# The far path's tables loaded during the last batch, and four of six lead rows evicted by VectorE, in a two-block convolution kernel

## The reference

```
x = x + L0(group_norm(x))     # two 3x3 conv branches, each times a sigmoid attention map
x = x + L1(group_norm(x))     # modulated deformable 3x3 convolution, batch norm, relu

def L1(x):                                    # K*K = 9 taps
    off_y, off_x = conv3x3(x, offset_w)       # one offset per tap and pixel
    mask = 2 * sigmoid(conv3x3(x, mod_w))
    sy, sx = off_y + row + tap_y, off_x + column + tap_x
    sampled = bilinear(x, sy, sx) * mask      # zero outside the image
    out = einsum('nckhw,ock->nohw', sampled, weight) + bias
    out = (out - mean) * rsqrt(var + 1e-5)    # over batch and pixels
    return relu(out * gamma + beta)
```

## Time and profile before

| | us |
|---|---|
| runs, median (lowest to highest of 3) | 423.75 (423.46 to 424.14) |
| profiled execution | 425.59 |
| its span | 423.8 |

### The profile page before, as it was taken

The page is one execution under the profiler, slowest core; times in us unless marked ns, Lnnn a source line. Parts: engine busy times, 40 slices in busy tenths (PEclk is TensorE's granted clock), DMA queues, the critical chain, the costliest instruction groups (busy, mean ns, idle before and its releaser), DMA issues.

```text
span 423.8 us, 14386 instructions
## 1 busy us (share of the span) xinstructions
PE 313.0 (74%) x6057; PEld 203.1 (48%) x6058; DVE 319.8 (75%) x625; ACT 252.8 (60%) x380; POOL 204.3 (48%) x242
## 2 busy tenths in 40 slices
PE   0079999848747419899989989898998999870470
PEld 0022334312213106777757777677775777760460
DVE  5456267833689852999979999799999799993266
ACT  1023322405047108888888888788888888880355
POOL 9770000199491001666646665556666466656000
PEclk9999999969679558999999999999999999996565
DMA  7799200178580643300011001001100000000005
GB/s 226 131 234 239 48 2 0 26 212 235 128 208 9 128 97 90 97 28 3 29 29 44 6 28 28 29 11 40 29 29 26 4 5 3 3 4 19 2 0 198
DMA packets 18106, 28.65 MB, mean 68 GB/s; under 512 B 6890, under 2 KB 7465, under 8 KB 18029
## 3 DMA queue, kind: packets, MB, share of 16 engines
q1 hardware_dynamic: 12397, 19.40, 17.1%
q0 software_dynamic: 2400, 5.07, 5.2%
q10 hardware_dynamic: 3246, 3.27, 3.5%
HBM read 8.03 MB, written 5.83 MB: 33 GB/s over the span
## 4 chain that ended last, share of the span: by engine, by line
PE 42%; ACT 28%; DVE 8%; DMA 7%; SPq 6%; issue 5%; ACTq 1%; POOL 1%; DVEq 1%; POOLq 0%
ACT hx L931 17%; PE ps L641 10%; PE ps L771 9%; ACT zreg L1014 8%; PE ps L584 6%; PE ps L605 5%; PE ps L654 4%; DMA hx<-xpad 3%; SPq L440 3%; PE ps L595 2%; SPq L345 2%; ACT zreg L999 2%; PE ps L780 1%; DMA x_sb<-in_x 1%; DVE x_sb L1397 1%
## 5 line engine op out<-in xcount | busy, mean ns | idle before, releaser
L561 POOL TENSOR_TENSOR prod<-prod 128x416 f32<-128x416 f32 x128 | 134.9, 1075 | 119.4 <-DVE prod L1311 119.4
L1311 DVE TENSOR_TENSOR prod<-ps,hy 128x480 f32<-128x480 f32 (+1 forms) x256 | 137.6, 600 | 23.7 <-PE ps L780 20.9
L780 PE MATMUL ps<-zreg,hx 64*64 64x96 f32 x4608 | 113.1, 247 | 0.0
L931 ACT ACTIVATE hx<-ps 128x576 f32<-128x576 f32 x131 | 78.2, 648 | 49.2 <-PE ps L771 28.5
L780 PEld LDWEIGHTS ps<-zreg,hx 64*64 64x64 f32 x4608 | 101.0, 132 | 7.5
L1018 ACT ACTIVATE hx<-hx,rbias 128x1152 f32<-128x1152 f32 x64 | 81.1, 1267 | 0.0
L1319 DVE TENSOR_REDUCE areg<-prod 128x32 f32<-128x448 f32 x128 | 72.7, 608 | 0.5 <-POOL prod L561 0.4
L641 PE MATMUL ps<-preg,sel 26*128 26x288 bf16 x260 | 42.4, 281 | 31.0 <-ACT zreg L1014 18.1
L771 PE MATMUL ps<-wzp,sreg 128*128 128x144 bf16 x512 | 43.1, 227 | 0.0
L641 PEld LDWEIGHTS ps<-preg,sel 26*128 26x128 bf16 x260 | 19.9, 91 | 46.5 <-issue 31.0
L1014 ACT ACTIVATE zreg<-ps 128x576 f32<-128x576 f32 x64 | 42.1, 658 | 0.0
(11 more groups left out here) (178 smaller groups left out, 354.9 us busy)
## 6 DMA issues: line engine op xcount, KB each, us to landing
scratch<-zreg SPq DMA_DIRECT2D x12, 240.0 KB, 4.2
sreg<-scratch SPq DMA_DIRECT2D x12, 192.0 KB, 2.5
out<-x_sb SPq DMA_DIRECT2D x8, 256.0 KB, 2.1
x_sb<-in_x SPq DMA_DIRECT2D x3, 512.0 KB, 4.9
areg<-xpad POOLq DMA_DIRECT2D x23, 66.0 KB, 3.6
areg<-xpad SPq DMA_DIRECT2D x23, 66.0 KB, 2.7
sreg<-scratch SPq DMA_DIRECT2D x4, 336.0 KB, 3.3
zreg<-xpad POOLq DMA_DIRECT2D x15, 66.0 KB, 4.1
```

Source lines behind the costliest of these rows:

```text
L561: pool.tensor_tensor(slots[:, :, 0:2 * moved], slots[:, :, 0:2 * moved], slots[:, :, 2 * KEPT:6 * KK], ALU.add).then_inc(folded, 1)
L780: return pe.matmul(g_ps(g, h)[u * W:(u + 1) * W, k - TAPS[h][0], :, :], hx[s, (t + u) % 4, k, :], z_sb[s, y + u + k // 3:y + u + k // 3 + ...
L931: act.activation(hx[:, t % 4, :, :].rearrange("p k (h x) -> p h k x", h=2), dist_ps(bank).rearrange("p h (k x) -> p h k x", k=KK), ACT.Abs)\
L1311: mul = vector.tensor_tensor(pv[:, n0:n1], gv, wv[:, n0:n1], ALU.mult)
```

## The change

`far_tab` now begins at column 0 of `zreg`, in z rows 0 to 7. POOL clears it in four pieces of 544 columns, one after the folds of each of the pairs 54 to 57. These are pairs 6 to 9 of the last batch, which work on row 12 and later, so rows 0 to 7 are no longer read. SyncE's six loads wait for four pieces. As `out_t` now overlaps the tables, ScalarE waits for `far_loaded` ahead of its first output eviction. Of the six lead rows of a batch, VectorE evicts the first four (`lead_rows`, counted by `lead_low`), and ScalarE the last two (`lead_saved`).

```diff
--- before.py
+++ after.py
@@ -156,7 +156,7 @@
         xparts = zflat[:, ZSLOTS * KW - NPART * ZSLOTS * W:ZSLOTS * KW].bitcast(bf16)\
             .rearrange("p (q n) -> p q n", q=NPART)
         xrest = prod[:, :, :].rearrange("p a n -> p (a n)")[:, HH * B * KK:HH * B * KK + ZPIECE * P128]
-        far_tab = zflat[:, NPIX:NPIX + B * KW + 2 * B * P128]
+        far_tab = zflat[:, 0:B * KW + 2 * B * P128]
         wz_far = far_tab[:, 0:B * KW].rearrange("p (b n) -> p b n", b=B)
         sel_far = far_tab[0:SELK, B * KW:].bitcast(bf16).rearrange("p (e n) -> p e n", n=P128)
         out_t = zflat[:, 0:NPIX]
@@ -241,6 +241,7 @@
         zrow_saved = sem("zrow_saved")
         lead_made = sem("lead_made")
         lead_saved = sem("lead_saved")
+        lead_low = sem("lead_low")
         dist_made = sem("dist_made")
         dist_ready = sem("dist_ready")
         g_ready = sem("g_ready")
@@ -310,6 +311,7 @@
             return ps[:, (bank + u) * BANK:(bank + u) * BANK + KW]
 
 
+        DVE_LEADS = 4
         LEAD_BANKS = (0, 0, 2, 2, 0, 0)
 
         def pair(row):
@@ -356,6 +358,7 @@
 
         FAR = H + 2
         FAR1 = 128
+        FAR_PIECES = 4
 
         def far_rows(eng, tile, turn):
 
@@ -473,7 +476,7 @@
                     sync.wait_ge(xs_loaded, b * (32 * NQ) + 32 * q)
                     sync.sem_inc(load_turns, 1)
                     load_piece(b, q)
-            sync.wait_ge(far_zeroed, 2)
+            sync.wait_ge(far_zeroed, FAR_PIECES)
             for b in range(B):
                 sync.dma_start(wz_far[b * C:(b + 1) * C, b, :], d["wz"]).then_inc(far_loaded, 16)
             for h in range(2):
@@ -560,10 +563,11 @@
                     moved = 3 * KK - KEPT
                     pool.tensor_tensor(slots[:, :, 0:2 * moved], slots[:, :, 0:2 * moved], slots[:, :, 2 * KEPT:6 * KK],
                                        ALU.add).then_inc(folded, 1)
-
-            pool.wait_ge(acc_ready, NT)
-            pool.memset(far_tab[:, 0:B * KW], 0.0).then_inc(far_zeroed, 1)
-            pool.memset(far_tab[:, B * KW:], 0.0).then_inc(far_zeroed, 1)
+                piece = i - (NT // 2 - HH // 2 + 6)
+                if 0 <= piece < FAR_PIECES:
+                    n = (B * KW + 2 * B * P128) // FAR_PIECES
+                    pool.memset(far_tab[:, piece * n:(piece + 1) * n], 0.0).then_inc(far_zeroed, 1)
+
             pool.wait_ge(reach_ready, 2)
 
             pool.wait_ge(px_ready, 16 * (1 + 3 * PX_DMAS))
@@ -748,7 +752,7 @@
                 for j in range(ZLEAD):
                     if j >= 4:
 
-                        pe.wait_ge(lead_saved, b * ZLEAD + (j - 3))
+                        pe.wait_ge(lead_low, b * DVE_LEADS + (j - 3))
                     z_row(j, j % 2, LEAD_BANKS[j]).then_inc(lead_made, 1)
                 for y in range(0, HH, 2):
                     t = b * HH + y
@@ -761,7 +765,8 @@
                     pe.wait_ge(dist_ready, t + 3)
                     pe.wait_ge(zrow_saved, t + CREDIT)
                     if y == 0:
-                        pe.wait_ge(lead_saved, (b + 1) * ZLEAD)
+                        pe.wait_ge(lead_low, (b + 1) * DVE_LEADS)
+                        pe.wait_ge(lead_saved, (b + 1) * (ZLEAD - DVE_LEADS))
                     for u in range(2):
                         distance((t + 2 + u) // HH, (t + 2 + u) % HH, PAIR_BANKS[u])
 
@@ -994,7 +999,7 @@
             for b in range(B):
 
                 act.wait_ge(xparts_stored, 16 * B * (NQ - 1))
-                for j in range(ZLEAD):
+                for j in range(DVE_LEADS, ZLEAD):
                     act.wait_ge(lead_made, b * ZLEAD + (j + 1))
                     act.activation(z_sb[:, j, :], z_ps(j % 2, LEAD_BANKS[j]), ACT.Copy).then_inc(lead_saved, 1)
                 for y in range(0, HH, 2):
@@ -1040,6 +1045,8 @@
             act.activation(warm[:, 5:6], warm[:, 0:1], ACT.Sqrt).then_inc(warmed, 1)
             for c in range(NCH):
                 act.wait_ge(outt_made, c + 1)
+                if c == 0:
+                    act.wait_ge(far_loaded, 16 * (B + 2))
                 act.activation(out_t[:, c * BANK:(c + 1) * BANK], ps[:, (c % 4) * BANK:(c % 4 + 1) * BANK],
                                ACT.Identity, bias=vec[:, V_DBIAS:V_DBIAS + 1]).then_inc(outt_saved, 1)
             root(4)
@@ -1320,9 +1327,18 @@
                                      .rearrange("p (a n e) -> p a e n", a=C // 2, e=2)[:, :, :, 0:KEPT],
                                      AX.X, ALU.add).then_inc(acc_ready, 1)
 
+            def lead_rows(b):
+
+                for j in range(DVE_LEADS):
+                    vector.wait_ge(lead_made, b * ZLEAD + (j + 1))
+                    vector.tensor_copy(z_sb[:, j, :], z_ps(j % 2, LEAD_BANKS[j])).then_inc(lead_low, 1)
+
+            lead_rows(0)
             for i in range(NT // 2):
                 weigh(i, 0)
                 weigh(i, 1)
+                if (i + 1) % (HH // 2) == 0 and i + 1 < NT // 2:
+                    lead_rows((i + 1) // (HH // 2))
                 if i > 0:
                     add_up(i - 1, 0)
                     add_up(i - 1, 1)
```

## The result

| kernel | median of its runs (lowest to highest) | ratio to before | profiled execution, span |
|---|---|---|---|
| before, same chip | 423.94 (423.46 to 428.67) | 1 | 425.59, 423.8 |
| after | 420.41 (417.69 to 424.10) | 0.9874 (0.9825 to 0.9923) | 424.10, 422.3 |

The kernel is faster by 1.26%, with an interval of about 0.5% to either side; 419.4 us and 1.0% were forecast. All ratios here are taken over undisturbed runs alone, which leaves out the profiled execution of after (424.10, the slowest of its four). The quotient of the two medians is 420.41 / 423.94 = 0.9917, so the size of the gain is known less well than the first number suggests.

A forecast was written before the change was run, and what follows sets the result against it. The prediction took a chain of waits as the bound, ScalarE and TensorE alternating in the pair loop, the tail waiting for its tables. Early tables -4.82 and lead rows +0.45 made -4.37: 423.75 to 419.4 us, range 417.8 to 421.2.

The forecast's parts named there:

- the case's own: Whole kernel: the narrower range given for the main forecast itself, 418.9 to 420.0 us, chance 65%.
- TensorE's path after the last reduce: Entry to far loop: last reduce ends 384.23, loop entry 385.35, `L808` at 386.17, `L818` at 387.33.
- The register work's 0.82: TensorE's far-loop entry: 0.82 us of sequencer work before the first matmul, kept from behind the table's landing.
- POOL's path: Far-loop staging: POOL's sequencer enters at about 381.55, as the last folds start; its twelve copies end 5.49 later, at 387.04.
- Forecast slack 0.3: At `L818`: POOL's copies end at 387.04, 0.3 us ahead of TensorE's 387.33, so TensorE decides.
- Rival A: Far-loop staging: last folds hold POOL's sequencer, copies end 388.0 to 389.1, tail gain only 4.1 to 3.05; 13%.
- Part 1's additions: Last batch: four memsets in POOL's idle 1.14, SyncE's six DMAs near 364 and one ScalarE wait cost zero.
- Lead rows: Batch boundaries: VectorE evicting four of six rows costs +0.15 us at each of three, +0.45 in sum; first batch zero.
- 0.12 to its end in PSUM and 0.12 to ScalarE's start: Batch boundary: estimated handover of TensorE's lead row 5 to ScalarE's eviction, after two matmuls of 0.15.
- The price of a copy: VectorE's lead-row eviction at a boundary: 288 columns take 0.45 us, spaced 0.367 apart, 0.067 above the columns.
- Rival B: Tail: TensorE's full clock returns sooner, output chunks gain a further 0.7 to 1.0 us, giving 418.5; 14%.
- everything behind `L818` moves as a block: Tail: all work after `L818` shifts by the same amount, so the gain there is 4.82 us.

The follow-up runs named there:

- e7: The changed kernel with POOL's wait for all 128 reductions put back ahead of its far loop, no memset there; 422.40 us, ratio 0.9972.
- e8: The changed kernel with TensorE entering the far loop once VectorE's last multiply has freed PSUM, not after the last reduce; 420.53 us, ratio 0.9920.
- parts 1 and 2 alone: Two kernels against before: only the early tables, 419.62 us (ratio 0.9872); only VectorE's lead-row evictions, tables late, 425.19 us (ratio 1.0010).
- e4: The changed kernel with 24 unused matmuls over 26 rows, 512 columns, in TensorE's wait ahead of the first distances; 421.77 us, ratio 0.9921.
- part 1 alone: Before with only the early tables, ScalarE evicting all six lead rows; 419.62 us, ratio 0.9872; measured again 418.62 us, ratio 0.9849.
- after again: The changed kernel unaltered, measured again beside before; 419.05 us, ratio 0.9854.
- e5: The changed kernel with 30 unused matmuls over 128 rows, 288 columns, in TensorE's wait ahead of the first distances; 420.99 us, ratio 0.9916.
- e9: Early tables only, plus TensorE's earlier far entry, 32 unused matmuls behind the last taps and 30 ahead of the output transposes; 416.68 us, ratio 0.9825.
- e6: The changed kernel with 32 unused matmuls over 128 rows behind the last taps and 26 ahead of the output transposes; 419.03 us, ratio 0.9862.

## Why the prediction was right

- **Sum and time.** Forecast 419.4, measured 420.41 and, of the same kernel again on another chip, 419.05, both in the range of 417.8 to 421.2, the first outside the case's own 418.9 to 420.0. In ratios: 419.38 / 423.75 = 0.990 forecast, 0.9874 and 0.9854 measured (0.992 and 0.986 as quotients of the medians). The mechanism holds; that the size came so close is in part luck, as the next points show.
- **TensorE's path after the last reduce.** 1.94 from the last reduce to `L808` was forecast (386.17 - 384.23), 1.92 came. To `L818` 3.10 was forecast and 3.17 came, since the four matmuls between took 1.25 instead of 1.16. The register work's 0.82 could be carried over from where it stood behind a DMA.
- **POOL's path.** The sequencer was to pass while the last folds ran: it did, 0.1 behind the first one's start, and e7 shows what hangs on it. Forecast slack 0.3, measured 0.23 by e8 (in after `L823` starts 390.86 - 390.50 = 0.36 behind the copies' end, of which 0.15 is the handover). Rival A came only in e7, which was built to bring it about.
- **Part 1's additions.** Zero was right: four memsets of 0.54 in POOL's idle 1.14, and the DMAs at 368.1 to 370.3, with nothing behind them (the 364 of the forecast plus the 3.52 by which this execution's last folds start later, 385.01 against 381.49).
- **Lead rows.** +0.45 was forecast and +0.34 measured (0.44 in my split), but even so much is luck in its parts. A boundary costs 0.02 to 0.03, not 0.15: the step "0.12 to its end in PSUM and 0.12 to ScalarE's start" was too dear. From the last row's load to the distances I had 0.30 + 0.24 + 0.44 + 0.14 = 1.12, and 220.31 - 219.30 = 1.01 came; the load itself came 2.93 behind the multiplies' start, forecast 2.95. Three boundaries come to 0.07 where 0.45 stood. The first batch costs nothing, as forecast: the taps start 7.18 behind the distances in parts 1 and 2 alone, and 7.09 in before and e8. And the slow pair, 0.27, stood in no term.
- **The price of a copy.** The row gives 0.446 (forecast 0.45), and four in 1.54 makes a spacing of (1.54 - 0.446) / 3 = 0.365 (forecast 0.367), so 0.065 over the columns' 0.30. The Trainium skill (Perfetto Trace Analysis, Optimizing Scalar/DVE Operations) would have some 0.125 there for VectorE on PSUM; the trace does not bear that out. Its sentence changes no number here.
- **Rival B.** It came in part, by execution, and its chance of 14% was too low. The 32 transposes took 6.46 to 6.65 in all four executions with late tables. With early tables and no fillers in the tail they took 6.50 to 6.64 in after, e4 and e8, the three with a dip, 6.03 in e7, and 5.68 to 5.83 in part 1 alone (twice), after again and e5; the clock was at 0.74 over the stretch in part 1 alone. After and after again are one program and stand on either side. So tails with early tables and no fillers (e7 apart) differ by 0.9 (33.7 to 34.6), and the tail's gain is 5.0 to 5.9 rather than 4.82: "everything behind `L818` moves as a block" did not hold.

```profile
396.00:404.00 8.00, 5.68 (x32) 5.45 (x32) 5.51 (x9) 5.18 (x8) 0.00 (x0) 0.74 0.00 0
```

- **What it lacked.** The spread. I took 0.2% as what can be told from no change; the kernel before ranged over 1.5% in 23 runs, and the loop's start from 153.5 to 158.9 in executions that share all code ahead of it. Three runs within 0.16% had looked like a steady kernel. And I had no rival in which a stretch of full clock is lost elsewhere: profiled after lost some 2.9 against its own forecast of 421.2, 0.27 at the start, 1.75 in the first pair and 1.06 in the loop, with 0.2 won in the tail. The dips (after, e4 and e8, three of the seven executions that have both parts; none of the seven others) may belong to both parts together or to chance; that wasn't settled. In all three the clock falls 4.3 to 4.4 behind the first lead row of batch 3, and after and after again show that the program alone does not decide. Low clocks are not peculiar to the changed kernel: 4 of the 55 executions of before beside the experiments have a mean granted clock of 0.893, as profiled after has, but where these lost it is not on record.

## What to carry to other kernels

A load that only the tail needs belongs where its memory falls dead, but the gain is set by the next path: price each engine's own way from its last wait to the shared step, since here the sequencers ran ahead of their engines until the first wait that held, and one wait there was worth over 2 us. Sharing evictions between two engines brought nothing here, where the chain alternates with the engine that fills the banks. Where TensorE idles ahead of a serial tail, filler matmuls over all 128 rows that end shortly before the work can give back the clock, but count them so that they never outlast the wait: 24 in e4 and 30 in e9 did. Judge that by the stretch in the trace, for medians of six runs do not separate 0.5%. And before explaining a shift in a split of the trace, check that the split's own edge has not moved.

## What was not expected of the hardware

- 24 unbroken matmuls over 26 rows and 512 columns left the granted clock at 0.50 for 10.41 us; 30 over 128 rows and 288 columns raised it to 1.00 within 4.90.
- In e6 fillers of 4.09 behind the last taps kept the clock up over the following 2 of idleness: `L813` then ran in 0.81 rather than 1.25.
- ScalarE's 320th instruction costs 0.28 in every kernel in which it is the one that the chain waits for, and nothing where it is another; 8192 bytes of instructions are fetched right behind it.
- The same kernel, part 1 alone, needs 8.37 in one execution and 10.13 in another from the distances to the first multiply, because in the second the clock is back at 1.00 only 11.4 behind the first distances instead of 5.6: the next distances take 1.11 instead of 0.65, the z rows 1.14 instead of 0.67 and the taps 3.21 instead of 1.77.
